# A message-passing network on one core: the source rows that SyncE and ScalarE load one by one go back to GpSimd's gathers

## The reference, cut to what matters

```
h = x @ enc_W + enc_b                                   # 12500 nodes, 64 features
for l in range(3):
    cat = concatenate([h[src], h[dst], edge_attr])      # 212500 edges, sorted by dst
    m = relu(cat @ msg_W1[l] + msg_b1[l]) @ msg_W2[l] + msg_b2[l]
    agg = segment_sum(m, dst)
    h = gru_cell(agg, h, gru_Wih[l], gru_Whh[l], ...)
y = relu(h @ ro_W1 + ro_b1) @ ro_W2 + ro_b2
out = layernorm(x + y)
```

## Time and profile before

| what | value |
|---|---|
| median of three runs | 6155.57 us |
| the profiled execution, first to last instruction | 9775.6 us |
| GpSimd (POOL) busy | 4639.2 us |
| VectorE (DVE) busy | 3532.6 us |
| TensorE (PE) busy | 2880.1 us |
| ScalarE (ACT) busy | 346.4 us |
| indirect gathers of line 798 with a duration | 4767, mean 955 ns |
| DMAs of single rows | 9792 on SyncE's queue, 9792 on ScalarE's |

### The profile page before, as it was taken

The page is one execution under the profiler, slowest core; times in us unless marked ns, Lnnn a source line. Parts: engine busy times, 40 slices in busy tenths (PEclk is TensorE's granted clock), DMA queues, the critical chain, the costliest instruction groups (busy, mean ns, idle before and its releaser), DMA issues.

```text
span 9775.6 us, 72182 instructions
## 1 busy us (share of the span) xinstructions
PE 2880.1 (29%) x7290; PEld 1610.2 (16%) x7290; DVE 3532.6 (36%) x4656; ACT 346.4 (4%) x542; POOL 4639.2 (47%) x4865
## 2 busy tenths in 40 slices
PE   3323322322322332222222222223232222322223
PEld 2111111111111221111111111112111111111112
DVE  2333333333333433333333333333333334333334
ACT  0000000000000000000000000000000000000001
POOL 5444444444444454444444444445454445545543
PEclk6555555555555555555555555555555555555555
DMA  3111111111111111111111111111111111111111
GB/s 87 31 31 30 30 30 30 28 31 30 31 30 30 30 28 30 30 30 30 30 30 29 30 30 27 30 31 30 30 31 31 30 30 34 31 31 31 31 30 25
DMA packets 351443, 308.63 MB, mean 32 GB/s; under 512 B 149364, under 2 KB 237518, under 8 KB 350568
## 3 DMA queue, kind: packets, MB, share of 16 engines
q0 software_dynamic: 155328, 159.79, 8.6%
q1 hardware_dynamic: 118271, 110.17, 4.0%
q10 hardware_dynamic: 77328, 33.96, 1.4%
HBM read 280.52 MB, written 22.83 MB: 31 GB/s over the span
## 4 chain that ended last, share of the span: by engine, by line
SPq 57%; issue 38%; DVE 2%; PE 1%; another core or an unknown queue 1%; DMA 0%; ACT 0%; POOL 0%; DVEq 0%; ACTq 0%; POOLq 0%
SPq L473 46%; SPq L469 6%; SPq L642 2%; SPq L633 1%; SPq L527 1%; DVE work_ps L1493 1%; SPq L630 1%; DVE folds L1528 0%; DVE p_src L1490 0%; PE bank L838 0%; DMA p_src<-p_tab 0%; PE work_ps L949 0%; PE bank L962 0%; SPq L662 0%
## 5 line engine op out<-in xcount | busy, mean ns | idle before, releaser
L798 POOL DMA_INDIRECT p_src<-p_tab,idx_all x4767 | 4551.1, 955 | 4916.8 <-DVE work_ps L1493 3467.4
L962 PE MATMUL bank<-hot,folds 128*128 128x96 f32 x2496 | 660.1, 413 | 4012.9 <-issue 2053.0
L1490 DVE TENSOR_TENSOR p_src<-work_ps,p_src 128x512 f32<-128x512 f32 x624 | 427.6, 685 | 3374.9 <-DMA p_src<-p_tab 2912.1
L962 PEld LDWEIGHTS bank<-hot,folds 128*128 128x128 f32 x2496 | 532.1, 296 | 4278.5 <-issue 2198.0
L949 PE MATMUL work_ps<-w_edges,msg 128*128 128x512 f32 x1248 | 1120.0, 997 | 21.4 <-DMA windows_sb<-q_tab 21.4
L1523 DVE SCALAR_TENSOR_TENSOR work_ps<-work_ps,rel 128x1024 f32<-128x1024 f32 x624 | 768.8, 1232 | 21.5
L1493 DVE TENSOR_TENSOR work_ps<-p_src,bank 128x1024 f32<-128x1024 f32 x624 | 767.0, 1229 | 21.4
L1528 DVE TENSOR_REDUCE folds<-work_ps 128x256 f32<-128x1024 f32 x624 | 758.4, 1215 | 0.0
L959 PE MATMUL bank<-hot,counts 128*34 128x96 bf16 x416 | 68.9, 261 | 2248.6 <-issue 1278.6
L1538 DVE TENSOR_TENSOR sums<-bank,sums 128x96 f32 x624 | 158.1, 253 | 872.6 <-remote 699.5
L959 PEld LDWEIGHTS bank<-hot,counts 128*34 128x34 bf16 x416 | 27.1, 108 | 2368.2 <-issue 1359.8
(11 more groups left out here) (167 smaller groups left out, 1800.9 us busy)
## 6 DMA issues: line engine op xcount, KB each, us to landing
p_src<-p_tab ACTq DMA_DIRECT2D x9792, 0.2 KB
p_src<-p_tab SPq DMA_DIRECT2D x9792, 0.2 KB
p_src<-p_tab,idx_all POOLq DMA_INDIRECT x4830
msg<-in_edge_k SPq DMA_DIRECT2D x156, 256.0 KB
pick<-rel_tab SPq DMA_DIRECT2D x312, 96.0 KB
windows_sb<-q_tab ACTq DMA_DIRECT2D x312, 24.0 KB
windows_sb<-q_tab SPq DMA_DIRECT2D x312, 24.0 KB
pick<-q_tab ACTq DMA_DIRECT2D x312, 24.0 KB
```

What stands on the lines that cost most here:

```text
L798: pool.indirect_dma_start(out=p_src[r][0:rows, t, :], out_offset=None, in_=p_tab[l][0:NODES, :], in_offset=bass.IndirectOffsetOnAxis(ap=id ...
L962: last = nc.tensor.matmul(fold_ps, folds[:, b, :], hot_all[n % 2][:, s * BLOCKS + b, 1:WINDOW + 1], start=(b == 0), stop=(b == BLOCKS - 1))
L1490: nc.vector.tensor_tensor(rows, edge_ps[k % 2], rows, ALU.add).then_inc(with_edge, 1)
```

## The change

Every tile is gathered by GpSimd. Gone are the rows on SyncE and ScalarE, the loading of their nodes (`src_single`, one DMA on SyncE), the multiplication that turns these into byte offsets (one VectorE instruction, with its wait for the stored tables), the waits for the offsets, and VectorE's two waits for rows in the 153 steps. The seven row buffers, the early gathers and everything else stay.

```
         def gathers_of(m):
 
-            return LAST_TILES if m == STEPS - 1 else EDGE_TILES - has_singles(m)
-
-        def has_singles(m):
-
-            return m % GROUP == GROUP - 1 and m // GROUP < SINGLES
-
-        def single_rows(eng, kind, l, m, first, n, landed):
...
-            for at in range(first, first + n, PIECE):
...
-                for p, start in enumerate(starts, at):
-                    eng.dma_start(p_src[k % ROW_SLOTS][p:p + 1, SINGLE_TILE, :].bitcast(U8),
-                                  table[bass.ds(start, ROW_BYTES)].unsqueeze(0)).then_inc(landed[nth_single(l, m) % SINGLE_SEMS], 16)
...
+            return LAST_TILES if m == STEPS - 1 else EDGE_TILES
...
-                    if l == 0:
-                        sp.wait_ge(offsets_made, 1)
                     for g in range(2, GROUPS):
-                        single_rows(sp, mybir.EngineType.SP, l, GROUP * (g - 2) + GROUP - 1, 0, SP_ROWS, sp_singles)
                         group_inputs(n0 + g, g)
                         group_windows(l, n0 + g, g)
...
-                    single_rows(sp, mybir.EngineType.SP, l, STEPS - 1 - GROUP, 0, SP_ROWS, sp_singles)
...
                         for c, j in chunk_stages(m):
                             fast_chunk(l, c, j)
-                        for at, q in pieces_at(m):
-                            single_rows(act, mybir.EngineType.Activation, l, at, SP_ROWS + q * PIECE, PIECE, act_singles)
...
-                if has_singles(k % STEPS):
-                    n = nth_single(k // STEPS, k % STEPS)
-                    dve.wait_ge(sp_singles[n % SINGLE_SEMS], 16 * SP_ROWS * (n // SINGLE_SEMS + 1))
-                    dve.wait_ge(act_singles[n % SINGLE_SEMS], 16 * (128 - SP_ROWS) * (n // SINGLE_SEMS + 1))
...
-                dve.wait_ge(nodes_raw, 16)
-                all_stored(dve, 0, FAST_CHUNKS)
-                nc.vector.tensor_scalar(offsets, raw_nodes, float(ROW_BYTES), None, ALU.mult).then_inc(offsets_made, 1)
```

More of the change, by code:

```diff
@@ L8 @@
 U32 = mybir.dt.uint32
-U8 = mybir.dt.uint8
 ALU = mybir.AluOpType
@@ L67 @@
 ROW_SLOTS = 7
[L68 to L75, removed]
 PAIRS = CHUNKS // 2
@@ L191, in build @@
         both = pre_all[:].rearrange("p s g f -> p (s g f)")
-        raw_nodes = zr[0:GROUPS, 0:128].bitcast(I32)
-        offsets = p_src[ROW_SLOTS].rearrange("p t f -> p (t f)")[0:GROUPS, 0:128].bitcast(I32)
         src_seen = [dst_flat[:, 0:STEP], both[0:LATE_ROWS, :].bitcast(I32)]
@@ L303, in build @@
         gathered = [sem(f"gathered{s}") for s in range(GATHER_SLOTS)]
[L304 to L307, removed]
         early_in = sem("early_in")
@@ L571, in _ @@
                     sp.dma_start(idx_all[:, PRE:, :], io["src"][:, PRE:, :]).then_inc(idx_all_in, 16)
-                    sp.dma_start(raw_nodes, io["src_single"]).then_inc(nodes_raw, 16)
             sp.wait_ge(first_done, 1)
@@ L1201, in _ @@
                         windows_ahead(l, GROUPS * l + g, g)
-                    if l == 0:
-                        act.wait_ge(offsets_made, 1)
                     for m in range(STEPS):
@@ L1698 @@
         "src": src.transpose(2, 0, 1, 3).reshape(128, STEPS, EDGE_TILES),
-        "src_single": src[GROUP - 1::GROUP, BLOCKS - 1, :, RUN - 1],
         "src_early": src[0:EARLY].transpose(0, 1, 3, 2).reshape(EARLY, STEP),
```

## The result

The changed kernel takes 6345.67 us (four runs, 6343.74 to 6346.11), the kernel before 6155.17 beside it (four runs, 6152.11 to 6167.82): a ratio of 1.0306, 95% interval 1.0291 to 1.032. It is slower by 190.5 us. The forecast was 6344.

A forecast was written before the change was run, and what follows sets the result against it. GpSimd's gather list, at 1.2564 us a gather, was taken to bound the kernel: 6155.6 + 191.0 for added gathers - 3 at the start = 6343.6, say 6344 us (+3.1%), range 6302 to 6360.

The forecast's parts named there:

- The profiled wait that was not in the timed run: SyncE's row loads: 63.5 us a group when profiled, against 39.5 in timed runs, so most of the row time was discounted.
- 152 gathers at 1.2564 us, 191.0: GpSimd's list: of 153 added gathers one costs nothing, the other 152 lie on the path and add 191.0 us.
- the 13.3 us stop: GpSimd's wait between the 31 early gathers and the rest, 13.3 us, in which one added gather would be free.
- The budget of before: GpSimd's list in the kernel before, without waits on rows, summed to 6166.6 us against the timed median of 6155.6.
- The borders: Layer borders: GpSimd has 23.3 us, sixteen early gathers fill 21.0, leaving twice 2.3 = 4.6 us.
- The end: Kernel's end: 22.9 us from VectorE's last L1490 plus an assumed 2 us for a gather to land, 24.9 us.
- The start, -3 us out of 0 to 16: Step 10 reuses step 3's buffer; without its late rows GpSimd saves between 0 and 16 us, taken as 3.
- Costed at nothing: Removed rows, register loads, offset multiplication, nodes DMA and VectorE's waits: all hidden or off the path, 0 us.
- A: Rows partly late in timed runs too, GpSimd idling w us: 6344 - 1.03 w, 6246 at w = 95; chance 0.07.
- B: Rows bound the timed run; break even at 1.218 us a gather, 6066 us at 1.20, 1.5% faster; chance 0.04.
- C: A gather costs its transfer, not its issue: 153 gathers bring 27 us, 6182 at most; chance 0.01.
- D: Dearer than forecast: 6600 if every gather cost 1.315, or a few us per layer border, 6360 to 6370; chance 0.02.

The follow-up runs named there:

- experiment 11: Kernel before with single rows in every second group only, 75 more gathers, on chip 15: 6249.97 us, ratio 1.0154 to the kernel before.
- experiment 10: Changed kernel without the 153 gathers of each group's last tile and without rows for them, on chip 15: 6152.46 us, ratio 0.9997 to the kernel before.
- experiment 8: Changed kernel with every gather after the first four steps replaced by three GpSimd memsets, on chip 12: 5936.76 us, ratio 0.6083 to the kernel before.
- experiment 4: Changed kernel with most gathers fetching 128 bytes a row instead of 256, on chip 5: 7555.07 us, ratio 0.7707 to the kernel before.
- experiment 12: Changed kernel with most gathers bringing 64 rows instead of 128, on chip 15: 6129.27 us, ratio 0.9959 to the kernel before.

## Why the prediction was right

**The profiled wait that was not in the timed run.** The step on which everything hung was to set aside a chain and a wait list that both said "SyncE". It held: on a free chip the 64 rows take 25 us of a 39.5 us loop (experiment 11), and taking them away gives 0.03%, less than the interval (experiment 10). Only its wording, "a different machine state", was vaguer than what is true. Being profiled does not make the difference: timed runs on three chips show it too. On those chips the first reading, "taken at its word, the rows are the bound", is the right one, and the change wins 23%. The argument that settled it, one loop of the profile times the number of loops against the timed median, is good for the chip that the median came from and for no other. The prediction also laid the swelling of SyncE's queue to the rows ("Without rows there is nothing that swells SyncE's queue"). That is wrong: on chip 6 the window loads take up to 12.6 us with no rows at all, and the gathers are the cause (experiment 8). That the span came out near 6358 is luck in this respect: on chip 6 the span of the same kernel is 7548.4.

**152 gathers at 1.2564 us, 191.0.** The term is right in price: the distance of plain gathers in the changed kernel is 1.2564, and 190.5 us were measured as the whole difference. The count is one short: the eighth gather of step 3 was free because it would fall into the 13.3 us stop, and where the kernel takes 6155 there is no stop. So 153 gathers lie on the path, 192.2 us.

**The budget of before closed, but with errors that cancel.** Against the first gather at 42.5 (measured 42.6), the stop of 13.3 us after the first four steps' gathers is absent in the changed kernel's profile, and in that of experiment 10 too: in the trace of before the encoder's stores to `q_tab` were themselves held up, the last issued at 95.0 us against 67.7. The borders cost 6.9 and 0 us beyond the gap, not 2.3 each. The end is 32.7 from the last gather's start, not 26.2: VectorE's last `edge_sums` was taken to start 3.3 us after that start, 2 of them for landing, and it starts 10.0 us after it, behind GRU work of VectorE. (The 2 us had no row; the page of the changed kernel gives 2.8 us in the median from issue to landing.) With the changed kernel's terms before comes to 42.6 + 4829 x 1.2564 + 9.4 + 32.7 = 6151.9, and with 1.7 between span and time 6153.6, against 6155.2 measured: by this sum the rows cost it 1.6 us at most. The sum was 0.2% off before it was closed by lowering the distance; part of those 11 us belonged to the terms, part to the distance, and that 1.2564 then came out to the last digit is luck. The sum also counts 4830 distances where 4830 gathers have 4829 between them and the last one's own length, which makes no difference.

**The start, -3 us out of 0 to 16.** Not shown apart. The measured 190.5 is 1.7 below 153 x 1.2564 = 192.2, and experiment 10 is 2.1 below the kernel before; both lie within the intervals of their ratios. A saving of 1 or 2 us at the start would fit, and so would none.

**Costed at nothing.** Right: with SyncE's and ScalarE's rows, their register loads and VectorE's waits gone, the only thing that can be measured on a free chip is GpSimd's longer list.

**The rivals.** A (rows partly late) would have put experiment 10 at 6155 less w; 6152.46 leaves a w of about 2 us, and 7 at most by the interval. (Two sums of the rivals are slightly off: the 6064 us of gathers in A are 4830 x 1.2564 = 6068, and D's 6600 is 6640.) B (rows bound the timed run, distance below 1.218) is refuted on free chips by the distance; on held-up ones the rows do bound the kernel, with the same distance: before at 9800, changed at 7553. The 0.90 us of the earlier trace rows, which B tried as the length of every gather and which the prediction explained by GpSimd stopping behind it, belongs to the gathers of 20 rows; two of the three are followed by the next gather after the usual 0.30. C (transfer is the price, 6182 at most) falls with the result itself; the gather's length at half the bytes (952 ns, experiment 4) and the time at half the rows and bytes (216 us less in 4919 gathers, experiment 12) say the same. The sentence of the Trainium skill, "DMA: Bandwidth & Descriptors", section "Issuing engines are not separate DMA queues", holds in its first half; that the issue is "usually small relative to the DMA itself" is not so for these gathers, 1.256 us a piece against a queue busy 14.4% of the span, 914 us / 4983 = 0.18 us each. (One takes 2.8 us in the median from issue to landing, but these overlap with the gathers behind it.) D: from one plain gather to the next no more than 1.2564 in the mean; of its few us at each layer border 6.9 came at one and none at the other.

**What was to be seen in the profile.** GpSimd busy 4770 (forecast 4760), three quarters of the span; VectorE 3546 (3530); L1432 waiting 2529 us (2.6 ms) in 584 steps; waits of GpSimd for VectorE none (below 50); chain on GpSimd. The span was forecast at 6358 with 1.2587 a gather; it is 6344.0.

## What to carry to other kernels

Compare the span of the profiled execution with the timed median before you read any wait. Where they disagree by half, take from the trace only what is the same in both (counts, lengths of instructions, distances in a stretch without waits), and see whether some engine's list of instructions alone fills the median; if one does, that engine sets the time, and a change costs what it adds to that list.

An indirect gather costs GpSimd its instruction, hardly its rows or bytes (0.90 us with 20 rows, 0.95 with 128): at these sizes save gathers, not bytes. Loading rows one by one on other queues is a fair trade while these have idle time, here 0.32 us a row; but it is a trade whose result turned from +3% to -23% with the chip.

## What the runs showed of the hardware that was not expected

The stream of indirect gathers holds up the other engines on some chips. While GpSimd gathers without a pause, SyncE's loads stretch from 0.32 us a row to 2.5 (the profile of before) and from 1.83 us for four windows to 12.6 (chip 6) and 11.2 (chip 12), and VectorE and TensorE show waits of up to 28 us that end at nothing in the profile (chip 6); memsets of the same length on GpSimd do none of this (experiment 8). On chip 15 and the chip of the result the same stream leaves the others alone. The gather's own distance is 1.26 us on all of them.

It is not the loads alone that are stretched. Ahead of each row's DMA stands a small MOVE record, which issues no DMA, and it is stretched just as much. SyncE's, in the stretch of before in which GpSimd gathers (590 to 606 us); then over the whole run, for before on chip 6 and for half of the row steps on chip 15 (duration in ns min/median/max):

```profile
L473 SPq MOVE p_src<-p_tab x6: 690/690/729, 590.3 to 605.1; - x6
```
```profile
L473 SPq MOVE p_src<-p_tab x9792: 2/29/1409, 137.7 to 9744.7; - x200
```
```profile
L473 SPq MOVE p_src<-p_tab x4992: 29/29/38, 86.5 to 6162.4; - x200
```

On the free chip a MOVE is 29 ns; in the stretch of gathers MOVE and DMA alike are 0.7 us, and from one MOVE to the DMA behind it are 1.4 us. No MOVE on SyncE or ScalarE is longer than 43 ns in the profiles of the changed kernel and of experiments 8, 10, 11 and 12, while each of the other nine profiles has hundreds over 500 ns. That holds for the profile of before too, so it was held up in the same way. Half the bytes (experiment 4) made no difference either. This speaks for something on the way to or in the engines' carrying out of instructions, and against the path of the rows' data as the only one; it is argued and not shown, and by what path the gathers reach it, no run here tells. Nor is it known what sets the chips apart, or whether it is the chip at all: each of the four chips of the experiments was used for one set of runs only.

No kernel was found that is best on both kinds of chip: before wins by 3% on the free ones, the changed kernel by 23% on the others.
